# A mixture-of-experts layer on one core: the scatters of the routing notes behind the gathers, paced by the first product

## The reference, cut to what matters

```python
x = x + tanh(g_xattn) * fp8_blockwise_matmul(layernorm(x), ctx)      # x: 4 x 512 x 512
xr = layernorm(x).reshape(2048, 512)
probs = softmax(xr @ Wg)                          # 8 experts
gate_vals, expert_idx = top_k(probs, 2)           # two experts a row
pos = place of the row in its expert's list;  kept = pos < 640
for each expert e:                                # up to 640 rows each
    h = relu(xr[list of e] @ w1[e])               # 512 -> 2048
    rows += gate * (h @ w2[e])                    # 2048 -> 512
x = x + tanh(g_ffn) * rows
```

## Time and profile before

| | |
|---|---|
| time, median of 3 runs | 927.94 us (927.7 to 931.45) |
| the profiled execution | 930.51 us, of which the span of its instructions 928.8 us |
| TensorE busy | 829.3 us, 89% of the span, mean granted clock 0.962 |
| VectorE, ScalarE, GpSimd busy | 611.9, 364.3, 231.5 us |
| first product of expert 0 / of expert 1 | from 179.97 / from 305.22 us |
| the 32 scatters of notes | 32.4 us busy, first at 186.8 us |

### The profile page before, as it was taken

How to read it: one execution, slowest core, us unless ns; L and a number is a source line. 1 busy time by engine, 2 the same in 40 slices (tenths; PEclk the granted TensorE clock), 3 DMA queues, 4 the chain that set the end, 5 groups by cost and what they waited for, 6 DMA issues and landing times.

```text
span 928.8 us, 12104 instructions
## 1 busy us (share of the span) xinstructions
PE 829.3 (89%) x4279; PEld 392.8 (42%) x4280; DVE 611.9 (66%) x995; ACT 364.3 (39%) x584; POOL 231.5 (25%) x208
## 2 busy tenths in 40 slices
PE   0169998774699999999999999999999999999996
PEld 0134755431244444444444444444444444444442
DVE  4999889651559578678857585749574867484530
ACT  3889994221313344142424043413341334134410
POOL 2043331277122303321330223022302220222010
PEclk9999897696799999999999999999999999999998
DMA  8600633652338626543762636273627352602000
GB/s 300 245 0 1 227 136 114 218 146 45 103 103 182 205 90 174 209 147 119 186 210 104 158 106 211 101 158 119 209 90 169 132 187 90 169 23 68 1 25 22
DMA packets 79033, 123.16 MB, mean 133 GB/s; under 512 B 43134, under 2 KB 43150, under 8 KB 74912
## 3 DMA queue, kind: packets, MB, share of 16 engines
q1 hardware_dynamic: 68032, 93.33, 32.1%
q0 software_dynamic: 10976, 29.50, 11.2%
HBM read 96.52 MB, written 18.95 MB: 124 GB/s over the span
## 4 chain that ended last, share of the span: by engine, by line
PE 81%; DVE 11%; another core or an unknown queue 3%; issue 3%; ACT 1%; DMA 1%; POOL 0%; DVEq 0%; POOLq 0%; ACTq 0%
PE mm L786 36%; PE mm L856 35%; PE mm L559 3%; PE mm L765 2%; PE mm L826 1%; DVE region L1222 1%; DVE region L1211 1%; DMA gains<-in_g_ffn 1%; DVE region L1253 1%; DVE region L1249 1%; DVE region L1271 1%; DVE bn L1193 1%; DVE bn L1275 1%; PE mm L587 1%
## 5 line engine op out<-in xcount | busy, mean ns | idle before, releaser
L856 PE MATMUL mm<-region,w_split 128*128 128x512 f16 x1536 | 342.2, 386 | 28.1 <-issue 16.2
L786 PE MATMUL mm<-region 128*128 128x512 f16 x1536 | 336.0, 379 | 0.6 <-issue 0.6
L856 PEld LDWEIGHTS mm<-region,w_split 128*128 128x128 f16 x1536 | 152.0, 99 | 217.0 <-issue 30.7
L786 PEld LDWEIGHTS mm<-region 128*128 128x128 f16 x1536 | 148.9, 98 | 181.2 <-issue 4.4
L1130 ACT ACTIVATE region<-mm 128x512 f16<-128x512 f32 x128 | 76.4, 597 | 343.7 <-PE mm L856 285.8
L1582 DVE SCALAR_TENSOR_TENSOR region<-mm,region 128x512 f16<-128x512 f32 x128 | 88.5, 692 | 135.8 <-ACT region L1130 114.6
L478 POOL DMA_INDIRECT out<-region,back_now x40 | 64.0, 1599 | 169.4 <-DVE region L1595 140.2
L1585 DVE SCALAR_TENSOR_TENSOR region<-w_stage,w_scale,region 128x512 f16<-128x512 f32 x128 | 96.2, 752 | 0.0
L1133 ACT ACTIVATE region<-w_stage,w_scale 128x512 f16<-128x512 f32 x128 | 91.2, 712 | 0.0
L455 POOL PARTITION_ALL_REDUCE peak_all<-peak x14 | 4.8, 345 | 315.7 <-DVE peak L1346 284.7
L1375 DVE SCALAR_TENSOR_TENSOR w_split<-w_stage,w_scale,w_split 128x2048 f16<-128x2048 f32 x32 | 75.3, 2394 | 1.8 <-DVE region L1611 1.7
(11 more groups left out here) (201 smaller groups left out, 592.3 us busy)
## 6 DMA issues: line engine op xcount, KB each, us to landing
w_stage<-in_L_ffn_w SPq DMA_DIRECT2D x64, 1024.0 KB, 5.4
region<-in_x SPq DMA_DIRECT2D x4, 1024.0 KB, 13.7
x_split<-region SPq DMA_DIRECT2D x8, 512.0 KB, 2.8
out<-region SPq DMA_DIRECT2D x4, 1024.0 KB, 6.2
w_stage<-in_ctx SPq DMA_DIRECT2D x2, 1024.0 KB, 13.1
region<-in_ctx SPq DMA_DIRECT2D x2, 1024.0 KB, 15.6
region<-x_split,row_next POOLq DMA_INDIRECT x40, 7.6
region<-out,row_next POOLq DMA_INDIRECT x40
```

What stands on the lines that cost most here:

```text
L786: mm = pe.matmul(mm2[s % 2][:, :], hidden[:, hh, f, s * P:(s + 1) * P], w2_split[:, wh, f, :], start=(f == 0 and hh + wh == 0), stop=(f == ...
L856: mm = pe.matmul(products(f), w1_split[:, wh, k, f * P:(f + 1) * P], xT[:, xh * KD + k, 0:WIDE], start=(k == 0 and wh + xh == 0), stop=(k ...
```

## The change

The five gathers of the old output rows now stand before the scatters. Each scatter, counted from 0, waits until a number of tiles of the first product of expert 0 is finished: (j - 4) * 2 // 3 + 1, at most 16, and no wait where that is zero or less (the helper `need` leaves it out then). So the scatters 0 to 3 don't wait, 4 and 5 wait for one tile, 6 for two, 7 and 8 for three, and so on, three scatters for two tiles; 27 to 31 wait for all 16.

```diff
+FREE_NOTES = 4
...
+            def note_after(j):
+
+                return (j - FREE_NOTES) * 2 // 3 + 1
+
             pool.wait_ge(q["split_out"], 32 * B)
             gather_x(0, first=True)
             pool.wait_ge(q["zeros_in"], 16)
             pool.wait_ge(q["notes_ready"], 1)
+            pool.wait_ge(q["rows_out"], 16 * B)
+            gather_acc()
             for i in range(NT):
                 for w in range(2):
+                    need(pool, q["mm1_done"], min(NF, note_after(2 * i + w)))
                     pool.indirect_dma_start(
                         lists, bass.IndirectOffsetOnAxis(ap=goals[:, w, i:i + 1], axis=0), notes[:, w, i, :], None,
                         bounds_check=E * C - 1, oob_is_err=False).then_inc(q["lists_out"], 16)
-            pool.wait_ge(q["rows_out"], 16 * B)
-            gather_acc()
             pool.wait_ge(q["lists_out"], 16 * 2 * NT)
```

## The result

The changed kernel takes 919.3 us (median of 5 runs, 918.5 to 922.2) against 929.06 us for the kernel before in the same measurement (5 runs, three of them those of the table ahead); the ratio is 0.990, with a 95% interval of 0.988 to 0.993. The profiled execution has a span of 917.6 us for 928.8. The prediction was 914.2, with a range of 905 to 931.

What follows compares the result with a forecast made beforehand. Late counts of finished tiles beside GpSimd's scatters were taken to bound the first product. Gain 276.0 - (248.6 + X) - 2.7 = 24.7 - X, with X 11: 13.7 us off 927.94, so 914.2, range 905 to 931.

Steps and rivals of the forecast that it cites:

- The hole and its place: Expert 0's first product, 77.7 us: TensorE's counts of finished tiles arrive late during GpSimd's run of scatters, the only candidate.
- X: Time the first product of expert 0 takes above a clean 44.0 us: 33.6 before, taken as 11 after; chance 0.47.
- reading (a): In the first product, lateness counts note scatters, so it starts 6.3 us later, with tile 9: 8.8 us over clean.
- (b): In the first product, lateness counts every DMA of GpSimd's queue, so it starts at tile 6 as before: 12.7 us.
- The tail: From the first product's end to TensorE's turns: held scatters, their landing, list's load, reduction, VectorE's work; 24.6 us.
- The landing behind the last scatter: On GpSimd's queue, the wait before the list's load, priced at 2.68 us from a later expert's row scatter.
- The one-time cost of the first reduction: On GpSimd behind the list's load: some 6.6 of the reduction's 7.68 us belong to the first call alone; all kept.
- The clock behind the stall: After TensorE's wait in front of the turns its clock falls, which costs 2.7 us.
- The sum: Whole kernel: the gain is 276.0 - (248.6 + 11) - 2.7, that is 13.7 us.
- the sentence that no other stretch has such a hole: Elsewhere at most six such DMAs run in a row, and no other slice behind the scatters' run has a hole.

Runs made afterwards that it cites:

- two repeated runs: The changed kernel, unchanged, run twice more on late chips: 918.1 us for 929.8 (ratio 0.986) and 919.9 us for 929.9 (0.989) of the kernel before.
- VectorE's order: Changed kernel with VectorE's two w2 peaks, first row tile's sum and rest's first piece ahead of its wait for the reduction: 885.8 us for 891.9 of the kernel before.
- the early reduction: Changed kernel plus one reduction of a constant called early, while GpSimd waits for the notes: 893.65 us for 891.9 of the kernel before, on a prompt chip.
- the notes out of bounds: Kernel before with every note's goal beyond the table, so scatters are issued but write nothing: 890.55 us for 892.4, on a prompt chip.

## Why the prediction was right, step by step

*The hole and its place*: right. The count of finished tiles is late, and not the work, and it is late only where a run of GpSimd's DMAs goes on. The pace cuts the run: the same 37 DMAs without it give the hole back in full, at 929.9 us. What was assumed of the pace held as well: the late counts were in 2.3 us behind the last DMA of the cut run, for the 2.5 taken.

*X*: 11 was taken, 54.2 - 44.0 = 10.2 was measured, and 13.7 and 14.0 in the two repeated runs on late chips. (On the prompt chips clean products took 43.0 to 43.5 us; against these every X is 0.5 to 1 us larger.) The two readings gave 8.8 and 12.7. The profiled run follows reading (a): the late tiles start with tile 8, not 9, and the last of them starts cold at 215.04. The repeated runs, late from tiles 5 and 6 on, lie nearer to (b). So neither reading is shown, and 11 between them was a middle value that happened to fit.

*The tail*: right in kind, 1.6 us too short: from the product's end to the turns 24.6 were predicted and 26.2 measured. The landing behind the last scatter is the term that was mis-sized: 4.86 us for the 2.68 taken from a row scatter. The five scatters took 6.9 for 6.1, and the load of the list and the reduction 7.3 for 8.6, so a part of the miss cancelled. The chain came onto the path as the prediction said: the product ends 23 us earlier and the last five scatters wait for its end. The place of the gathers is a smaller term that shows on prompt chips: behind the scatters they run while these land, and the list's load follows them at once or 0.83 us later; ahead of them they leave the landing bare. The wait before the turns is 4.12 us with them behind, in the run that wrote no notes, and 7.83 us with them ahead. The experiment on VectorE's order shows that this whole stall is one of queue order. The one-time cost of the first reduction is shown too: called early it took 6.19 us, and the call that VectorE waits for then followed the list's load at once. The Trainium skill ("GPSIMD Engine Reference", 2.1 Instruction dispatch) gives about 6 us for a first call, and the trace agrees.

*The clock behind the stall*: 2.7 predicted, 2.2 measured (from the turns to row tile 2's matmuls 10.7 us for 8.5). The 24 matmuls behind the stall took 7.07 us for the usual 5.35, some of them at the lower of the two levels, 1.2 in place of 2.4 GHz (granted clock 0.50 from 260.8 to 264.0 us, 1.00 from 266.0 on).

*The sum*: 24.7 - 10.2 = 14.5, less 1.6 for the longer tail and 0.4 for a product that started later (180.39 for 179.97), and 0.5 back from the clock, gives 13.0; the second expert starts 12.9 us earlier. The medians of the runs differ by 9.8 us. The two repeated pairs, with their larger X, differ by 11.6 and 10.0. Of the 3.9 us between 13.7 and 9.8, then, 0.8 had come up by the start of expert 1, where a landing too short was in part made up by the smaller X. The other 3.1 lie behind it, where the prediction had no term: 1.7 of them in the profiled pair's later experts.

*What was wrong*: the sentence that no other stretch has such a hole. The narrow matmuls of four later experts have gaps beside runs of only six DMAs, worth 1.7 to 2.7 us each on a late chip (4.4 in one case). The page's tenths don't show them. The stretch of expert 0's five gathers, ahead of the scatters, has a late result and gaps too, and its trace was there to be read. So a short run is not harmless, though no tile of the product was late beside the first scatters. And I took the lateness as a property of the kernel; it is one of the place where the kernel runs. That the result was measured on a late chip, like the trace that the prediction was read from, is luck. For a prompt chip the prediction has the wrong sign: the product is clean, the pace as written holds nothing (scatter 27 goes out at 223.38, behind the product's end at 222.5), so gathers first without pace is the same order there, and that was slower by 0.5%. The changed kernel itself ran on no prompt chip, so this last step is argued from near twins; the early reduction and VectorE's order, which have its pace and did run there, support it, since their scatters, with the gathers ahead, were held for 0.2 us in all.

*Open*: what delays TensorE's counts and, in narrow matmuls, its issue. It is not the size of the written notes. Whether it is the data writes at all, or the generation and completion of the DMAs, was to be told by the notes out of bounds, which met no late chip. The rows of expert 0's five gathers speak against the writes into HBM: these DMAs only read from HBM, and a result beside them is late all the same (7.95 us of waiting for 2.84). That the two latenesses have one cause is not shown. Nor is it known what distinguishes the chips.

## What to carry to other kernels

On two of the four chips a run of small DMAs from GpSimd held TensorE's signals and its narrow matmuls although the DMA engines were busy for a third of the time only. Look for waits that end with an unknown releaser while every other engine idles, give such a run gaps early, and don't leave the remainder in a block behind the stage. Compare kernels only on one chip. Before moving or holding work in a queue, ask what stands behind it: here a landing and the one-time cost of the first reduction came onto the path. A wait that nothing needs yet should stand behind the work that others need, which gave 6 us against the kernel before on a prompt chip, and together with the early reduction 17 us beyond the pace on a late one.

## What the runs showed of the hardware that was not expected

The same program takes 929.8 and 929.9 us on two chips and 891.9 and 892.4 us on two others, with no difference in work. From one first product to the next, expert 0 takes 123.5 and 125.1 us in two traces of the kernel before on a late chip and 97.5 on a prompt one (with the notes out of bounds), and four later experts about 91.4 for 89.0. Beside five gathers in a row the late chips already show a late signal and gaps in small matmuls. Between the end of the last note scatter's issue and the list's load 3.5 to 5.3 us passed in eight of the nine traces with the scatters last, on both kinds of chip, and 2.3 us in the ninth (gathers first without pace on a late chip), against 2.7 for a row scatter.
